# Per-head attention scores of layers 0, 2 and 3: contraction over a strip of 32 partitions in place of all 128

## The reference, cut to what matters

```python
# layer 0 feed-forward part, layer 2 and layer 3 cross-attention; 8 batches, H = 16 heads, d = 8
Q = split_heads(x @ Wq.T + bq)            # (B, 16, 256, 8)
K = split_heads(context @ Wk.T + bk)      # layer 0: of x itself
V = split_heads(context @ Wv.T + bv)
scores = einsum('bhsd,bhnd->bhsn', Q, K) / sqrt(8)
# layers 0 and 2: softmax over all 256 keys; layer 3: softmax over the 32 largest
out = einsum('bhsn,bhnd->bhsd', weights, V)
```

## Time and profile before

| | |
|---|---|
| Median of 3 runs | 2310.37 us (2308.21 to 2314.17) |
| The profiled execution, its own time | 2307.16 us |
| Its span | 2305.4 us |
| TensorE busy (matmul; weight loads) | 2055.2 us (89%); 1606.9 us (70%) |
| VectorE busy | 1951.0 us (85%) |
| ScalarE busy | 1476.1 us (64%) |
| POOL (GpSimd) busy | 948.3 us (41%) |
| Mean granted TensorE clock | 0.958 |

### The profile page before, as it was taken

How to read it: one execution, slowest core, us unless ns; L and a number is a source line. 1 busy time by engine, 2 the same in 40 slices (tenths; PEclk the granted TensorE clock), 3 DMA queues, 4 the chain that set the end, 5 groups by cost and what they waited for, 6 DMA issues and landing times. The chain is left out here.

```text
span 2305.4 us, 41495 instructions
## 1 busy us (share of the span) xinstructions
PE 2055.2 (89%) x12569; PEld 1606.9 (70%) x12569; DVE 1951.0 (85%) x7828; ACT 1476.1 (64%) x3637; POOL 948.3 (41%) x1374
## 2 busy tenths in 40 slices
PE   5879798989999899998999899898999899888677
PEld 3556577656986578766886579775887669767466
DVE  1289797998989898998989899898989989796982
ACT  3546367776676667686577667676677766468341
POOL 3232213554164534544155443544345541443441
PEclk9878889999999999999999999999999999899798
DMA  4000101000100101001100101001010001001000
GB/s 188 1 8 1 35 7 50 1 8 29 56 4 1 35 6 53 1 2 35 42 18 1 35 2 56 4 1 35 13 47 1 1 29 56 31 1 56 1 3 3
DMA packets 29503, 55.03 MB, mean 24 GB/s; under 512 B 2914, under 2 KB 10082, under 8 KB 28642
## 3 DMA queue, kind: packets, MB, share of 16 engines
q1 hardware_dynamic: 29282, 52.37, 7.0%
HBM read 51.31 MB, written 1.05 MB: 23 GB/s over the span
## 5 line engine op out<-in xcount | busy, mean ns | idle before, releaser
L265 DVE MATCH_REPLACE8 top_work<-top_eight,top_work 128x256 f32<-128x256 f32 x1664 | 666.9, 408 | 0.0
L267 DVE MAX8 top_eight<-top_work 128x8 f32<-128x256 f32 x1664 | 616.7, 412 | 0.2
L305 POOL TENSOR_TENSOR top_p<-top_p,top_rest 128x512 f32<-128x512 f32 x192 | 244.4, 1273 | 217.4 <-ACT top_rest L298 217.4
L850 PE MATMUL bank<-workP 128*128 128x256 f32 x1024 | 278.1, 396 | 9.1 <-POOL workP L1012 4.0
L990 ACT ACTIVATE att_pP<-bank,att_tinyP 128x256 f32<-128x256 f32 x512 | 215.2, 476 | 67.2 <-DVE att_tinyP L1039 66.4
L850 PEld LDWEIGHTS bank<-workP 128*128 128x128 f32 x1024 | 181.3, 194 | 55.7 <-issue 29.9
L1039 DVE TENSOR_REDUCE att_tinyP<-bank 128x2 f32<-128x512 f32 x256 | 172.6, 679 | 24.1 <-PE bank L850 23.0
L267 DVE MAX8 top_lead<-bank 128x8 f32<-128x256 f32 x384 | 144.6, 417 | 46.4 <-PE bank L645 22.7
L298 ACT ACTIVATE top_rest<-top_work,top_nmax 128x256 f32<-128x256 f32 x384 | 173.3, 503 | 10.6 <-DVE top_work L265 10.3
L273 POOL TENSOR_SCALAR top_nmax<-top_lead 128x2 f32<-128x2 f32 x192 | 37.5, 195 | 336.9 <-DVE top_lead L267 336.6
L1012 POOL TENSOR_SCALAR workP<-workP,const 128x256 f32<-128x256 f32 x256 | 122.3, 484 | 130.3 <-PE bank L850 94.4
(11 more groups left out here) (365 smaller groups left out, 4587.8 us busy)
## 6 DMA issues: line engine op xcount, KB each, us to landing
gelu_w<-in_pack3w SPq DMA_DIRECT2D x72, 256.0 KB, 3.0
top_qk<-in_pack3w SPq DMA_DIRECT2D x72, 256.0 KB, 2.8
pack<-in_pack SPq DMA_DIRECT2D x1, 4352.0 KB, 19.7
pack<-in_pack SPq DMA_DIRECT2D x1, 2266.0 KB, 9.8
pack<-in_pack SPq DMA_DIRECT2D x1, 1028.0 KB, 8.1
mix_wb<-in_ctx SPq DMA_DIRECT2D x1, 1024.0 KB, 4.9
x_in<-in_x SPq DMA_DIRECT2D x8, 128.0 KB, 2.1
ctx_tok<-in_ctx SPq DMA_DIRECT2D x8, 128.0 KB, 2.4
```

What stands on the lines that cost most here:

```text
L265: ins = nc.vector.match_replace(self.work[:, u % 2, j, :], eight, src, GONE)
L267: ins = nc.vector.max(eight, src)
L305: self.k.nc.gpsimd.tensor_tensor(v, v, self.rest[:, :, :], ALU.subtract).then_inc(*self.p_ready.one())
L850: mm = self.k.nc.tensor.matmul(self.banks[u % 2][:, j * T:(j + 1) * T], self.q1[:, u % self.RING, j * P:(j + 1) * P], self.kT, start=True, ...
```

## The change

`by_strip` reorders the output columns of Wq and Wk and their biases for the three attentions, so that heads 4a to 4a+3 no longer lie side by side: head u has its eight channels in strip u mod 4 (32 partitions each), at place u div 4 within the strip. `strip_rows` has four columns in place of sixteen: column a is one at place a of every strip. One masked copy of the queries thus holds four heads, one a strip, and the scores contract over the head's strip alone (32 partitions, `strip(u)`), where the other three places are zero in the queries. `PlainHeads` makes its four copies at once, when the queries are projected, into four slots that are not used again in the stage; `HeadsTop` makes two at its start and the other two after heads 3 and 7, into two slots. Values, output weights and everything behind the scores keep their order.

```diff
+def strip(u):
+    return slice(PAD * (u % NG), PAD * (u % NG + 1))
...
 class HeadsTop(TopSelect):
     def score(self, pe, u):
-        pe.wait_ge(*self.q1_ready.at(u + 1))
+        pe.wait_ge(*self.q1_ready.at(u // NG + 1))
...
-            mm = self.k.nc.tensor.matmul(self.banks[u % 2][:, j * T:(j + 1) * T], self.tops.q1[:, u % 2, j * P:(j + 1) * P],
-                                         self.tops.k3, start=True, stop=True)
+            mm = self.k.nc.tensor.matmul(self.banks[u % 2][:, j * T:(j + 1) * T], self.tops.q1[strip(u), u // NG % 2, j * P:(j + 1) * P],
+                                         self.tops.k3[strip(u), :], start=True, stop=True)
...
-    def pool_q1(self, pool, u):
-        if u >= 2:
-            pool.wait_ge(*self.scores.at(u - 1))
-        self.k.nc.gpsimd.tensor_scalar(self.tops.q1[:, u % 2, :], self.tops.q3, self.k.w["head_rows"][:, u:u + 1], 1.0,
+    def pool_q1(self, pool, a):
+        if a >= 2:
+            pool.wait_ge(*self.scores.at(NG * (a - 1)))
+        self.k.nc.gpsimd.tensor_scalar(self.tops.q1[:, a % 2, :], self.tops.q3, self.k.w["strip_rows"][:, a:a + 1], 1.0,
...
-        u = self.at(s, 0, 0) + 2
-        if 2 <= u < H:
-            self.pool_q1(pool, u)
+        u = self.at(s, 0, 0)
+        if u >= 0 and u % NG == NG - 1 and u // NG + 2 < HG:
+            self.pool_q1(pool, u // NG + 2)
...
 class PlainHeads(Units):
-    RING = 4
...
-        pe.wait_ge(*self.q1_ready.at(u + 1))
+        pe.wait_ge(*self.q1_ready.at(u // NG + 1))
...
-            mm = self.k.nc.tensor.matmul(self.banks[u % 2][:, j * T:(j + 1) * T], self.q1[:, u % self.RING, j * P:(j + 1) * P],
-                                         self.kT, start=True, stop=True)
+            mm = self.k.nc.tensor.matmul(self.banks[u % 2][:, j * T:(j + 1) * T], self.q1[strip(u), u // NG, j * P:(j + 1) * P],
+                                         self.kT[strip(u), :], start=True, stop=True)
...
         if s == 2:
             pool.wait_ge(*self.proj_copied.at(self.order.index("q") + 1))
-            for u in range(3):
-                self.pool_q1(pool, u)
-        u = self.at(s, 0, 0) + 3
-        if 3 <= u < H:
-            self.pool_q1(pool, u)
+            for a in range(HG):
+                self.pool_q1(pool, a)
...
+    by_strip = np.arange(D).reshape(HG, NG, HD).transpose(1, 0, 2).reshape(D)
...
-        "hsum": hsum.reshape(D, -1), "head_rows": np.kron(np.eye(H, dtype=f), np.ones((HD, 1), f)),
+        "hsum": hsum.reshape(D, -1), "strip_rows": np.kron(np.ones((NG, 1), f), np.kron(np.eye(HG, dtype=f), np.ones((HD, 1), f))),
```

More of the change, by code:

```diff
@@ L28 @@
 RF_SCALE = float(D) ** -0.25
-CONST = [("ident", 128), ("tri", 128), ("ones", 128), ("hsum", NG * 128), ("head_rows", H), ("group_rows", HG), ("group_eps", HG), ("part_rows", E16),
+CONST = [("ident", 128), ("tri", 128), ("ones", 128), ("hsum", NG * 128), ("strip_rows", HG), ("group_rows", HG), ("group_eps", HG), ("part_rows", E16),
          ("sim", E16), ("bq0", 1), ("bk0", 1), ("bq2", 1), ("bk2", 1), ("bq3", 1), ("bk3", 1)]
@@ L719, in pool @@
                 pool.wait_ge(*self.start.proj_copied.at(3))
-            for u in range(2):
-                self.pool_q1(pool, u)
+            for a in range(2):
+                self.pool_q1(pool, a)
         u = self.at(s, 0, 0)
@@ L1006, in act, with pool_q1 @@
             nc.scalar.activation(self.otT[:, :], b[2][:, 0:T], ACT.Copy).then_inc(*self.otT_ready.one())
[L1008 to L1012, removed]
+    def pool_q1(self, pool, a):
+        self.k.nc.gpsimd.tensor_scalar(self.q1[:, a, :], self.qT, self.k.w["strip_rows"][:, a:a + 1], 1.0,
                                        ALU.mult, ALU.mult).then_inc(*self.q1_ready.one())
@@ L2742 @@
         "part_rows": np.concatenate([np.tile(np.eye(E16, dtype=f), (PARTS, 1)), np.zeros((P - PARTS * E16, E16), f)]),
-        "rf": rf.reshape(D, -1), "wq0": w_qkv[:, 0:D], "wk0": w_qkv[:, D:2 * D],
+        "rf": rf.reshape(D, -1), "wq0": w_qkv[:, 0:D][:, by_strip], "wk0": w_qkv[:, D:2 * D][:, by_strip],
         "wv0": w_qkv[:, 2 * D:], "gate0": a["L0_ffn_W_gate"], "exp0": side_by_side(a["L0_ffn_W_experts"]),
-        "bq0": b_qkv[0:D].reshape(D, 1), "bk0": b_qkv[D:2 * D].reshape(D, 1),
+        "bq0": b_qkv[0:D][by_strip].reshape(D, 1), "bk0": b_qkv[D:2 * D][by_strip].reshape(D, 1),
         "wq1": a["L1_xattn_Wq"], "wk1": a["L1_xattn_Wkv"][:, :H1 * HD1], "wv1": a["L1_xattn_Wkv"][:, H1 * HD1:],
@@ L2760 @@
     for L in (2, 3):
-        for c in "qkvo":
+        for c in "qk":
+            parts[f"w{c}{L}"] = a[f"L{L}_xattn_W{c}"].T[:, by_strip]
+        for c in "vo":
             parts[f"w{c}{L}"] = a[f"L{L}_xattn_W{c}"].T
-        parts[f"bq{L}"], parts[f"bk{L}"] = (a[f"L{L}_xattn_b{c}"].reshape(D, 1) for c in "qk")
+        parts[f"bq{L}"], parts[f"bk{L}"] = (a[f"L{L}_xattn_b{c}"][by_strip].reshape(D, 1) for c in "qk")
         parts[f"bv{L}"], parts[f"bo{L}"] = (a[f"L{L}_xattn_b{c}"] for c in "vo")
```

## The result

The changed kernel takes 2475.59 us (median of 6 runs, 2457.76 to 2481.06) against 2310.19 us of the kernel before beside it (6 runs): a ratio of 1.070, interval 1.065 to 1.074. It is slower by some 165 us. The forecast was 2349 us, range 2322 to 2385: the direction holds, the size does not, and the result lies outside the range.

The account below looks back on a forecast made before the run. TensorE and VectorE nearly full; border costs less pairs pass 36 us in six rounds and 6 outside, less POOL's 3: +39 on 2307.2 us gives 2346, plus 3 for the median: 2349 us, range 2322 to 2385.

Parts of the forecast that it names:

- What bounds the kernel: TensorE 89% and VectorE 85% busy; TensorE sets layer 2's pace, neither has room in layer 0's stretch.
- The score itself: In each head's score on TensorE, 32 rows instead of 128 save nothing by themselves: 0 us.
- Changing the shape of the array: On TensorE around scores between 128*128 work, new borders cost 0.20 us entering, 0.14 leaving: 101 us in all.
- The shares let through: Per round 2.6 of 3.6 us (layer 2), 2.8 of 4.6 (layer 0), 0.6 of 3.1 (layer 3) reach the end.
- Scores side by side: At 19 places two heads' scores lie in different strips, each saving 0.77 us: 15 us of TensorE's time.
- Masked copies at nothing: On POOL 288 of 384 copies go, 139 us of its time, costed at nothing; earlier `keep_top` gains 3 us.
- all of it passes: Rival: all added TensorE time, +86 us, reaches the end through the fixed order, 2397 us; chance 0.12.
- VectorE covers: Rival: where VectorE is full it sets the pace, only layer 2's stretch and first block pass, 2323 us; chance 0.15.
- Bare weight loads: Rival: three loads per score cannot overlap matmuls of their own strip, 219 us more, about 2480 us; chance 0.02.

Follow-up runs that it names:

- k65: The changed kernel with every head's scores over partitions 0 to 64, 65 rows, without new borders: 2341.83 us, ratio 1.015.
- k128: The changed kernel with every head's scores over all 128 rows, copies and order as changed, no new borders: 2309.45 us, ratio 1.000.
- k64: The changed kernel with scores over two alternating halves of 64 rows, with borders: 2425.98 us, ratio 1.054.
- pairs: The changed kernel with two heads' strip scores issued back to back in layers 0 and 2, behind transposes and values: 2543.90 us, ratio 1.102.
- fill32: The changed kernel with one full-height 128x256 matmul in front of each head's strip scores, which overwrite it: 2660.68 us (four runs).
- border32: The changed kernel with scores over all 128 rows and one tiny 32-row matmul in front of each head's: 2432.80 us, ratio 1.054.

## Why the prediction was wrong

**The sum as it is now.** k65 spends 77 us more at half clock than k128 and takes 32 us longer, with no border: 0.42 us at the end for each us at half clock. The change spends 435 - 175 = 260 us more, which is 109 us; with 60 us for the borders that makes 169, where 166 us lie between it and k128. For k64 it is 144 x 0.42 = 60, and 59 for its 600 new borders: 119, measured 117. The changed kernel's own runs give nearly the same price: 2457.76 us at a clock of 0.917 and 2480.0 at 0.906, 22 us for 58 us more at half clock, 0.38. The 0.42 is an average of this program and holds where the order is the change's. Against their controls at full height, pairs lost 130 us where this sum would give some 200, and fill32 216 us (profiled executions) where it would give 168; in its layer 2 stretch the borders pass whole, not by 60 to 70%.

The forecast lay 126 us below the result. Of that an estimated 109 us are the clock, which it did not have, and 18 us the borders, 60 at the end where it let 42 through with the pairs taken off.

Step by step:

- *What bounds the kernel*: right. TensorE sets the pace of layer 2's stretch, both engines that of layer 0's; VectorE's wait for scores rose from 23.0 to 105.5 us.
- *The score itself, "fewer rows save nothing by themselves: 0 us"*: **this step failed.** It is true of a score at full clock, 1.05 us as in the earlier trace rows. But fewer rows are not free: with them TensorE's clock fell, for everything around the scores too. 260 us more at half clock, an estimated 109 us at the end, is the term that the sum lacked. I had taken the clock as given, read the earlier trace rows only to divide by two, and had no rival on the clock. The earlier trace rows has it at 0.90, 0.94 and 0.81 in three stretches of the kernel before, so it was a quantity that could move.
- *Changing the shape of the array, 0.20 us in and 0.14 out*: right: 1.05 and 0.50 as forecast, and the 5.2 us of sixteen heads in fill32 at full clock; border32 gives 0.27 for 0.34.
- *The shares let through*: right in the stretches, too small over the program. Layer 0's stretch grew by 2.8 us at full clock (2.8 let through), layer 2's by 2.7 in k64 at full clock (2.6 let through). Up to 1 us of layer 0's is luck: k128, which has no new borders, takes up to 45.0 us there from the first score to the last, the kernel before 44.0 to 44.6. All borders gave an estimated 60 us at the end; the forecast had 36 and 6 for borders and pairs together. The stretches outside the rounds passed more than my 6 us, or the pairs less; no run tells which.
- *Scores side by side, 0.77 us a pair*: the mechanism is right and the size a little low: two heads take 1.06 us where one takes 1.05, so the second saves nearly its whole 0.86. What it is worth at the end was not isolated.
- *Masked copies at nothing, +3 us gained*: right within what a measurement can tell. POOL is busy 135 us less (139 forecast) and k128, which has that relief alone, is level.
- *The rivals*: "all of it passes" (2397 us) and "VectorE covers" both took the border price as the whole. "Bare weight loads" came nearest in time (about 2480 us), by luck, for a reason that the rows exclude: a head's four records take 1.05 us with 0.2 us of loads each, so the loads do run beside matmuls of their own strip.

**What the clock answers to.** Not borders alone (border32: 0.964). Not idleness: at 0.80 TensorE is busy for 41.82 of 42.50 us, in fill32 at 0.58 for 69.30 of 69.30 (the ends of matmuls are modelled, but no row shows a wait). Not the values: before the change each masked copy of the queries was zero outside eight of its 128 partitions, and the clock was 1.00 in layer 2's stretch. What is left is the height of the scores, and the table is in that order. k65 shows it without borders, ahead of the rounds. In the rounds the clock of the stretches of layers 0 and 2 fell only with strips of 64 or 32 rows, where fewer rows, the borders, the smaller part of the array and the change from strip to strip come together; no run separates these. A kernel with `slice(0, 64)` for every head would take the last of them out and was not run. The Trainium skill, in "TensorE: Matmul & The Clock Gate", part The HAM clock gate, has the half clock follow how busy the engine has recently been, idle engines being held back. By that rule these stretches would all be at full clock; the trace disagrees, at 98% busy and 0.80.

**What stays open.** The same stretch runs at 1.00 in one round and at 0.80 or 0.58 in another of one execution (k64, fill32); what tips it is not settled. That slower work before it keeps the clock down would fit pairs, fill32 and the parts that do not add, but it is only argued. 32 rows without borders were not tried: here every operand of 32 rows had records of another array part than the work around it, so that borders came with it. No kernel here is faster than the one before.

## What to carry to other kernels

A matmul over fewer rows is not cheaper in time, and may cost clock: price it at its full-height duration plus a border on each side (here 0.20 us in, 0.14 us out), and read the granted clock of a trial run before trusting that sum. Where a trace has TensorE near full and its clock below 1.00 in some stretches, give the clock a rival of its own, for about 0.4 us at the end per us at half clock in a kernel bound as this one (0.46 in layer 2's stretch of fill32, which TensorE fills: 26.9 us for 58). To tell clock from price, run the same order at full height with the operand merely enlarged: one `slice(0, 128)` separated the two here.

## What the hardware showed that I had not expected

- TensorE's mean granted clock over the program goes down with the rows that its scores address: 0.962 at 128, 0.955 at 96, 0.946 at 65, 0.934 at 64, 0.912 at 32, with the same number of instructions. Borders stand in the last two alone.
- Two heads in different strips of 32 rows take 1.06 us, one takes 1.05; the order with the most such pairs has the lowest clock, 0.885.
- A new border costs 0.098 us at the end of this program (65 us for 661), some 60 to 70% of its 0.14 to 0.17 us on TensorE, at a clock that does not change.
- One full-height matmul in front of each head's strips leaves layer 2's stretch at full clock in three rounds of six; in one of the others the same work takes 69.3 us in place of 42.4, without a row that waits.
